# Full-height score matmuls in layers 1 and 3 of a four-layer attention and expert kernel, and full-width value matmuls in layer 1

## The reference

```
# layer 1, per sequence: 8 heads of 64 channels, INNER = 512
q = layer_norm(x) @ Wq ; k, v = split(layer_norm(ctx) @ Wkv)
sim = einsum('bhid,bhjd->bhij', q, k) * 64**-0.5      # 256 queries x 256 keys
out = einsum('bhij,bhjd->bhid', softmax(sim), v) ; y = out @ Wout + bout
# layer 3: the same with a rotary turn of the context's keys, and keys and values
# of the 256 positions of x itself behind those of the context: 256 queries x 512 keys
```

## Time and profile before

| | us |
|---|---|
| three runs, median | 1868.16 |
| lowest and highest | 1861.4, 1869.75 |
| the profiled execution | 1862.23 |
| its span on the core | 1860.5 |
| TensorE matmul busy in the span | 1693.1 (91%) |
| VectorE busy | 1091.3 (59%) |
| ScalarE busy | 681.6 (37%) |

### The profile page before, as it was taken

How to read it: one execution, slowest core, us unless ns; L and a number is a source line. 1 busy time by engine, 2 the same in 40 slices (tenths; PEclk the granted TensorE clock), 3 DMA queues, 4 the chain that set the end, 5 groups by cost and what they waited for, 6 DMA issues and landing times. The chain is left out here.

```text
span 1860.5 us, 28250 instructions
## 1 busy us (share of the span) xinstructions
PE 1693.1 (91%) x9431; PEld 1236.4 (66%) x9431; DVE 1091.3 (59%) x3250; ACT 681.6 (37%) x1747; POOL 258.4 (14%) x277
## 2 busy tenths in 40 slices
PE   6889778799998999999887799999889999999799
PEld 4667546567766568888676578887656665656575
DVE  5988866568787532232368571002356777676666
ACT  5877842454454211111133222221133443344331
POOL 2100131211022100000232120000120001010115
PEclk9999989999999999999899899999989999999999
DMA  8854042211012325454353875335221111011363
GB/s 250 254 184 134 7 128 68 80 37 36 28 58 81 110 90 170 153 165 169 102 170 117 292 285 176 114 124 176 57 86 43 43 44 50 26 35 29 103 190 113
DMA packets 170926, 212.91 MB, mean 114 GB/s; under 512 B 17081, under 2 KB 137506, under 8 KB 170658
## 3 DMA queue, kind: packets, MB, share of 16 engines
q1 hardware_dynamic: 159730, 183.57, 30.7%
q0 software_dynamic: 10496, 27.28, 4.6%
q10 hardware_dynamic: 560, 0.27, 0.1%
HBM read 148.95 MB, written 57.92 MB: 111 GB/s over the span
## 5 line engine op out<-in xcount | busy, mean ns | idle before, releaser
L788 POOL DMA_INDIRECT slots_in<-f_xn,f_slot x88 | 85.0, 966 | 465.1 <-DVE f_slot L562 441.3
L3506 PE MATMUL r_bank<-r_w,r_hT 128*128 x624 | 139.3, 379 | 1.0 <-DVE r_hT L3650 1.0
L3506 PEld LDWEIGHTS r_bank<-r_w,r_hT 128*128 128x128 f32 x624 | 118.4, 190 | 22.8 <-issue 7.5
L1498 ACT ACTIVATE a_probs<-a_s,a_negmax 128x512 f32<-128x512 f32 x128 | 86.9, 684 | 103.7 <-DVE a_negmax L1746 103.7
L1347 PEld LDWEIGHTS a_t<-kept_ident,a_probs 128*128 128x128 f32 x768 | 83.1, 142 | 61.8 <-issue 38.8
L1331 PE MATMUL a_s<-a_kT,a_qT 64*128 64x256 f32 (+1 forms) x512 | 109.1, 524 | 14.2 <-ACT a_probs L1504 7.6
L3591 DVE TENSOR_TENSOR r_y<-r_bank,r_b_row 128x256 f32<-128x256 f32 (+1 forms) x27 | 14.7, 543 | 177.5 <-PE r_bank L3506 177.2
L3121 PE MATMUL r_bank<-r_xgT,r_firsts 128*128 128x256 f32 x512 | 113.2, 379 | 0.0
L2283 DVE CUSTOM_DVE_ANT_0 a_s<-a_s,a_mask_bias 128x256 f32<-128x256 f32 x256 | 100.5, 454 | 20.3 <-PE a_s L2110 20.1
L1746 DVE TENSOR_REDUCE a_negmax<-a_s 128x1 f32<-128x512 f32 x128 | 82.2, 683 | 49.7 <-PE a_s L1331 49.1
L1347 PE MATMUL a_t<-kept_ident,a_probs 128*128 128x128 f32 x768 | 106.4, 281 | 2.0 <-DVE a_probsT L1764 1.6
(11 more groups left out here) (424 smaller groups left out, 3408.3 us busy)
## 6 DMA issues: line engine op xcount, KB each, us to landing
r_firsts<-in_f_w SPq DMA_DIRECT2D x27, 1024.0 KB, 5.1
r_firsts<-in_f_w SPq DMA_DIRECT2D x46, 512.0 KB, 4.3
slots_in<-a_zeros SPq DMA_DIRECT2D x8, 2048.0 KB, 12.6
half_in<-a_zeros SPq DMA_DIRECT2D x8, 1024.0 KB, 9.7
r_w<-in_f_w SPq DMA_DIRECT2D x8, 1024.0 KB, 7.0
a_share_of<-shares_out SPq DMA_DIRECT2D x28, 256.0 KB, 3.9
r_xg<-slots_in SPq DMA_DIRECT2D x28, 256.0 KB, 2.9
slots_out<-r_y SPq DMA_DIRECT2D x28, 256.0 KB, 2.1
```

The lines of the kernel that those rows point to most:

```text
L788: pool.indirect_dma_start(self.slots_in[:, :], bass.IndirectOffsetOnAxis(ap=self.slot[:, c, tile:tile + 1], axis=0), src, None).then_inc(s ...
L1498: last = nc.scalar.activation(probs[:, g % PROBS, i, :], bank[:, :], ACT.Exp, bias=negmax[:, g % 4, i, 0:1], accum_out=sum_of(e, h, t_only))
L3506: last = nc.tensor.matmul(d_bank[:, t * D:(t + 1) * D], hT[:, j % 2, m, t * P:(t + 1) * P], slots.second[:, bass.ds(e, 1), m, :], start=(m ...
```

## The change

1. **Queries beside zeros.** `qT` gets a copy per head: `qT[:, parity, g, block, :]` holds head g's channels in their 64 rows and zeros in the other 64. Two GpSimd memsets per layer clear the zero halves once. ScalarE writes only a head's own 64 rows, so what was one activation over 128 partitions is two over 64 partitions each.
2. **Scores over 128 rows.** The stationary tile is 128 x 128 and the moving one the whole `kT[:, parity, block, :]`, 128 rows. The zeros cancel the other head's rows. The first head's calls all come before the second head's.
3. **Layer 1's values beside zeros.** `v[:, parity, kt, block, g, :]` has 128 columns, head g's 64 and 64 of zeros. Four GpSimd memsets clear the zeros. VectorE moves the values by two copies of 128 x 256 in place of one of 128 x 512. Both heads add up in the whole `o_bank` in one accumulation of four calls. Layer 3's `weigh` stays as it was.
4. **Rotary keys.** The product with the cosine goes straight to `kT` and the sum is made in place; the buffer `k_cos` is gone.

The memsets stand on GpSimd behind the first gathers and ahead of `rotate_first`. ScalarE waits for `q_cleared` at the first q, TensorE for `v_cleared` at layer 1's first `weigh`.

```diff
-        qT = sb("qT", [P, 2, PACK, NC_, SEQ])
+        qT = sb("qT", [P, 2, GROUPS, NC_, SEQ])
-        v = sb("v", [P, 2, KT, H, VROW])
+        v = sb("v", [P, 2, KT, H, VROW] if WIDE else [P, 2, KT, BLOCKS, GROUPS, P])
-            k_cos = sb("k_cos", [P, 2, 2, SEQ])
@@ gpsimd, behind the gathers of GATHERS_AHEAD
+            for g in range(GROUPS):
+                others = slice((1 - g) * R, (2 - g) * R)
+                pool.memset(qT[others, :, g, :, :], 0.0).then_inc(q_cleared, 1)
+            pool.wait_ge(q_cleared, GROUPS)
+            if not WIDE:
+                for g in range(GROUPS):
+                    for e in range(2):
+                        pool.memset(v[:, e, :, :, g, (1 - g) * R:(2 - g) * R], 0.0).then_inc(v_cleared, 1)
             if cfg.rope:
                 rotate_first()
@@ tensor, scores
-                for t in (t_only,) if WIDE else range(TB):
-                    for i in range(2):
-                        g = 2 * pair + i
-                        rows = slice(g * R, (g + 1) * R)
-                        c, m = blk // PACK, blk % PACK
+                for i in range(2):
+                    for t in (t_only,) if WIDE else range(TB):
                         out = banks[i][:, :] if WIDE else banks[i][:, t * SEQ:(t + 1) * SEQ]
-                        last = nc.tensor.matmul(out, qT[rows, e % 2, m, c, t * P:(t + 1) * P], kT[rows, e % 2, c, :],
+                        last = nc.tensor.matmul(out, qT[:, e % 2, i, blk, t * P:(t + 1) * P], kT[:, e % 2, blk, :],
                                                 start=True, stop=True)
@@ tensor, weigh
+                elif not WIDE:
+                    pe.wait_ge(v_cleared, 2 * GROUPS)
                 for kt in range(KT):
                     for i in range(2):
...
+                        else:
+                            last = nc.tensor.matmul(o_bank[:, 0:SEQ], v[:, e % 2, kt, blk, i, :], probsT[:, half, i, kt, :],
+                                                    start=(kt == 0 and i == 0), stop=(kt == KT - 1 and i == 1))
@@ scalar, move of q
-                    last = nc.scalar.activation(qT[:, e % 2, 0, 2 * j:2 * j + 2, :],
-                                                bank[:, :].rearrange("p (c n) -> p c n", c=2), ACT.Copy, scale=cfg.scale)
+                    if e == 0 and j == 0:
+                        act.wait_ge(q_cleared, GROUPS)
+                    for g in range(GROUPS):
+                        own = slice(g * R, (g + 1) * R)
+                        last = nc.scalar.activation(qT[own, e % 2, g, 2 * j:2 * j + 2, :],
+                                                    bank[own, :].rearrange("p (c n) -> p c n", c=2), ACT.Copy, scale=cfg.scale)
@@ vector, rotary keys
-                    nc.vector.tensor_tensor(kT[:, e % 2, 2 * j:2 * j + 2, 0:SEQ], k_cos[:, j, :, :], k_turn[:, j, :, :],
-                                            ALU.add).then_inc(rope_done, 1)
+                    keys = kT[:, e % 2, 2 * j:2 * j + 2, 0:SEQ]
+                    nc.vector.tensor_tensor(keys, keys, k_turn[:, j, :, :], ALU.add).then_inc(rope_done, 1)
@@ vector, move of v
-                    last = nc.vector.tensor_copy(v[:, e % 2, j, :, :].rearrange("p h d -> p (h d)"), bank[:, :])
+                        for g in range(GROUPS):
+                            last = nc.vector.tensor_copy(v[:, e % 2, j, :, g, g * R:(g + 1) * R],
+                                                         bank[:, :].rearrange("p (b g d) -> p b g d", g=GROUPS, d=DV)[:, :, g, :])
```

More of the change, by code:

```diff
@@ L1005, in tiled_attention @@
         cT = sb("cT", [P, DK, SEQ])
-        qT = sb("qT", [P, 2, PACK, NC_, SEQ])
+        assert PACK == 1 and GROUPS == 2
+        qT = sb("qT", [P, 2, GROUPS, NC_, SEQ])
         kT = sb("kT", [P, 2, NC_, KEYS])
-        v = sb("v", [P, 2, KT, H, VROW])
+        v = sb("v", [P, 2, KT, H, VROW] if WIDE else [P, 2, KT, BLOCKS, GROUPS, P])
         probs = sb("probs", [P, PROBS, 2, 512])
@@ L1056, in tiled_attention @@
         max_ready = sem("max_ready")
+        q_cleared = sem("q_cleared")
         o_full = sem("o_full")
@@ L1067, in tiled_attention @@
         half = R // 2
-        v_cleared = sem("v_cleared") if PACK > 1 else None
+        v_cleared = sem("v_cleared")
         slots_zero = [sem(f"slots_zero{i}") for i in range(len(zeroed))]
@@ L1363, in weigh @@
                         h = blk * GROUPS + g
-                        last = nc.tensor.matmul(o_bank[g * R:(g + 1) * R, 0:SEQ], v[:, e % 2, kt, h, :],
-                                                probsT[:, half, i, kt, :], start=(kt == 0), stop=(kt == KT - 1))
+                        if WIDE:
+                            last = nc.tensor.matmul(o_bank[g * R:(g + 1) * R, 0:SEQ], v[:, e % 2, kt, h, :],
+                                                    probsT[:, half, i, kt, :], start=(kt == 0), stop=(kt == KT - 1))
+                        else:
+                            last = nc.tensor.matmul(o_bank[:, 0:SEQ], v[:, e % 2, kt, blk, i, :], probsT[:, half, i, kt, :],
+                                                    start=(kt == 0 and i == 0), stop=(kt == KT - 1 and i == 1))
                 if block_done(s) is not None:
@@ L1638, in move_prep @@
                     chunks = bank[:, :].rearrange("p (c n) -> p c n", c=2)
-                    for dst, turn in ((k_cos, cos), (k_sin, sin)):
-                        last = nc.vector.tensor_tensor(dst[:, j, :, :], chunks, turn[:, :].unsqueeze(1).to_broadcast([P, 2, SEQ]),
+                    for dst, turn in ((kT[:, e % 2, 2 * j:2 * j + 2, 0:SEQ], cos), (k_sin[:, j, :, :], sin)):
+                        last = nc.vector.tensor_tensor(dst, chunks, turn[:, :].unsqueeze(1).to_broadcast([P, 2, SEQ]),
                                                        ALU.mult)
@@ L1653, in move_prep @@
                 else:
-                    last = nc.vector.tensor_copy(v[:, e % 2, j, :, :].rearrange("p h d -> p (h d)"), bank[:, :])
+                    if WIDE:
+                        last = nc.vector.tensor_copy(v[:, e % 2, j, :, :].rearrange("p h d -> p (h d)"), bank[:, :])
+                    else:
+                        for g in range(GROUPS):
+                            last = nc.vector.tensor_copy(v[:, e % 2, j, :, g, g * R:(g + 1) * R],
+                                                         bank[:, :].rearrange("p (b g d) -> p b g d", g=GROUPS, d=DV)[:, :, g, :])
                 last.then_inc(t_free, 1)
```

2 lines of the change are left out of this document (1 added, 1 removed).

## The result

| | before | after |
|---|---|---|
| median of 4 runs, us | 1867.38 (1861.4 to 1869.75) | 1923.67 (1922.62 to 1925.49) |
| profiled execution, us | 1862.23 | 1922.62 |
| its span, us | 1860.5 | 1920.9 |

The kernel after is slower: ratio 1.0307, 95% interval 1.0282 to 1.0333, which is 56 us. The forecast was 1941 us (1918 to 1962), so the direction holds, the time lies in the range, and it is 17 us under the forecast. It is only 3.7 us above the 1920 of rival 1, *more is given back*, which had a chance of 0.08. The two profiled executions differ by 60.4 us; 4.9 of these lie in stretches that the change does not touch (the one of before was 5.9 us under its median), and 55.5 in the attention of layers 1 and 3. Those 55.5 are what has to be explained.

The account below looks back on a forecast made before the run. The prediction took TensorE to bound the kernel: +80.3 us of array time, -10 from waits and +2.5 in the openings gave +73, so 1941 us on the median of 1868.16, range 1918 to 1962.

Parts of the forecast that it names:

- rival 1: Whole kernel: waits give back twice as much (-20) and the openings' clock -8, so +52, 1920 us; chance 0.08.
- What bounds the kernel: Attention loops of layers 1 and 3: TensorE sets the pace, so its added time is added in the end, less its waits.
- What a half tile costs: Scores and `weigh`: two heads run side by side, eight half instructions taking 0.86 us plus 0.21 or 0.15 at the switch.
- rival 4: Half-tile groups: heads do not run side by side, so only switches are saved, 15 us per layer, 1838 us; chance 0.03.
- Rival 3: Score and `weigh` instructions: full-height weight loads are not hidden, 0.10 us each, +77 more, 2018 us; chance 0.03.
- The sum on TensorE: Scores of layers 1 and 3, `weigh` of layer 1: full tiles add 40.6 and 39.7 us, together +80.3.
- What the waits give back: TensorE's waits in layers 1 and 3 shrink as it comes later: -10 us, bounds -3 to -20.
- The clock: Opening stretches, granted 0.93 and 0.88: longer matmuls might keep it up, worth at most 11.7 us; taken as 0.
- The openings: Start of layer 1: q's second activation 1 us plus GpSimd holding up VectorE 1.5, together 2.5; layer 3 taken as 0.
- the lock: Layer 1's opening: q's GpSimd memsets hold up VectorE's normalising of x, 0 to 2.8 us, taken as 1.5.
- Other engines: ScalarE, VectorE, GpSimd: q's split adds 19 us on ScalarE, v's copies 2.8 on VectorE, mostly hidden; openings pay 2.5.
- signs that would have made the forecast wrong: Layer 1 scores plus `weigh` under 3 us, sequences growing under 3 us each, or `a_xn` over 4 us later at layer 1's opening.

Follow-up runs that it names:

- l3_half: The changed kernel with layer 3's scores back over each head's own 64 rows, rest kept: 1900.63 us, 1.0173 of the kernel before.

## Why the prediction was right, and where 17 us went

**What bounds the kernel** held: all three parts undone bring the loops back to within 1.1 and 0.6 us.

**What a half tile costs** held, and no longer rests on modelled ends: on the same rows or columns the groups last 1.92, 1.91, 1.87 and 3.60 us. That disposes of rival 4, as does `l3_half`, which gets its 22 us back with half tiles. Rival 3 (weight loads not hidden) is out too: full groups are 1.72 to 1.73 us, as priced. The sentence of the Trainium skill cited there (page "TensorE: Matmul & The Clock Gate", section "Part 3: Packing small matmuls — row/col tiling") would, taken alone, have given 77 us more; the full groups with 256 columns ran as closely spaced as before. The same section also lets a weight load run ahead into a background buffer, and with that the spacing agrees.

**The sum on TensorE** was 80.3 us and measures 77.4, since two switches were placed wrongly. A step of layer 1 goes from 0.10 + 1.01 + 1.07 + 0.93 (the transposes behind) = 3.11 to 1.73 + 1.73 + 0.87 = 4.33 us: +1.22, not +1.27. In layer 3 a step without `weigh` gains 1.72 - 0.10 - 1.06 - 0.06 = 0.50, not 0.55; one with it 1.82 - 1.06 - 0.06 = 0.70, not 0.69: `weigh` stayed at 1.88 and the switch showed in the scores behind it. 32 x (1.22 + 0.50 + 0.70) = 77.4. The step that failed here is in "what a half tile costs": that the loss at the end of a half group lies in that group alone. A tail of 0.06 us lies in the transposes behind.

**What the waits give back** is the term that was mis-sized. I took -10, by letting a third of the exponent waits go in layer 3, 2.0 of 7.6 us in layer 1, and half of layer 1's other idle time. TensorE's idle time in the two loops fell by 9.0 + 12.8 = 21.8 us, just past my bound of -20, which is also what rival 1 took. The rows: exponent waits at the scores 4.9 us less in layer 1 and 3.6 in layer 3 (I had 2.0 each), and then small waits spread over the loops that I had not gone through one by one. In layer 1 these two rows of the kernel before are gone:

```profile
PE a_t L1301 <- DVE a_probsT L1764: 1.3, 3, 0.8
PE a_s L1271 <- ACT a_probs L1504: 0.9, 1, 0.9
```

In layer 3 the last wait for `a_o_raw` fell by 2.1 us where I had 1.2, the waits for keys' DMAs fell from 2.3 to 1.0 us, for the router's x from 2.9 to 1.7, and one of 1.6 for `a_probsT` is gone. My reason for the third was that the exponent's chain starts at scores that end later. But VectorE and ScalarE start on the first bank. Where VectorE stood ready, its first maximum began 1.16 us behind the start of the scores before and 1.06 us after, 0.1 earlier (I had taken 0.2; behind `weigh` in layer 3 it is 1.16 in both). And TensorE arrives 1.2 us later at the next scores in layer 1 and 0.5 to 0.7 in layer 3. That this is what let them catch up is argued from these times and was not tried by itself; that later matmuls alone remove the waits and earlier ones bring them back is what `l3_half` shows.

**The clock** was taken at 0 and gave some. TensorE's busy time in the loops rose by 72.2 us, 5.2 less than the 77.4. In the loops of the kernel before, TensorE was busy for 16.6 us at a grant of 0.50, the 1.2 GHz level; after, for 10.0 us. At that level work takes twice as long, so this gave back (16.6 - 10.0) / 2 = 3.3 us. One stretch of each, before and then after:

```profile
1384.45:1391.28 6.83, 6.40 (x19) 4.39 (x20) 5.04 (x9) 3.31 (x10) 0.00 (x0) 0.50 0.58 219
...
1422.52:1425.93 3.41, 3.13 (x4) 1.40 (x5) 1.81 (x3) 2.04 (x7) 0.00 (x0) 0.50 0.77 304
```

The other 1.9 us are open; busy time rests on modelled ends. Rival 1 had the clock's gain in the openings, where layer 1's got worse; it came in the loops, and smaller.

**The openings** were taken at 2.5 us and measure 5.2 + 0. For the lock I took 1.5 of a possible 2.8; it cost 2.85, the upper bound, which is also the price by the Trainium skill's rule, and 1.6 more through the clock behind the longer wait, which I had not listed. That the bound was met so closely is partly luck: I had the whole of it in the normalising of x, which took 1.27 of it, while 1.58 came from the normalising of the context just ahead, which I had not counted. q's second activation cost 0.6, with 1 forecast. For layer 3 I took 0 between -1.8 and +1.8, and 0 it was, since one step was freed and another held.

The account: 77.4 - 3.3 (clock) - 1.9 (open) - 21.8 (idle) = 50.4 = 28.4 + 22.0 in the loops, and 5.2 in the opening, 55.6 for the 55.5 measured. Against the forecast's +73: -2.9 array, -3.3 clock, -1.9 open, -11.8 waits, +2.7 opening make -17.

So the cost, the bound and the place of the loss were right. That the time still fell into the forecast's own range of 1922 to 1953, 1.7 us above its lower end, owes something to luck: the waits went past their bound, and the openings, at 5.2 against a bound of 5, made up for a part of it. For the waits, rival 1 was the better forecast.

**Other engines.** An activation of q over 64 partitions takes 592 ns for 600 over 128, so its cost doubled as taken (64 of them, +19 us on ScalarE, hidden but for the 0.6). The halved copies of v take 414 ns each for 432 forecast. Both were hidden.

Layer 1's sequence was forecast at 33.9 us and is 33.4, layer 3's at 53.3 and is 52.5. Of the signs that would have made the forecast wrong none appeared.

## What to carry to other kernels

Two matmuls that stand on different halves of the array's rows or columns already share its time (for rows, in either order of issue); padding each with zeros to the full height saves the switches, about 0.1 to 0.2 us each, and pays a doubled group. When a tight loop's bound engine gets slower, go through all of its small waits: with 43 us of idle time in 632, half went away here, and with it a quarter of the 80.3 us that the array was to cost. A memset put on GpSimd for later use is not free: place it where VectorE runs no tensor_scalar on SBUF, above all behind the step on which TensorE is waiting.

## What the runs showed of the hardware

- Order of issue does not decide whether tiles of half height overlap (1.07 us both ways); their rows do (1.92 on the same rows). For half width the columns do (1.87 on the same, 1.01 on different ones). On the same rows or columns the group is the sum of its instructions plus 0.15 to 0.20 us of switch.
- From full tiles to half scores, and from half `weigh` to full scores, a switch costs about 0.10 us, seen in the full group (1.83 and 1.84 for 1.73). Leaving half scores for the transposes costs 0.21 us in the scores and 0.06 in the transposes.
- A wait of 4.24 us, where 1.29 had been, was followed by 3.8 us of matmuls at a mean grant of 0.56; so 2.9 us more of waiting cost 4.5.
- A memset on GpSimd holds a tensor_scalar of VectorE (two of 128x256: 2.38, 2.01 and 2.33 us, for 0.80 and 0.74 without it), and leaves alone a step of 128x2 with two inputs (0.16 us).
- An activation over 64 partitions takes as long as one over 128 (592 and 600 ns for 512 columns).
